# Weighted neighbour gather of one layer in two row tiles of TensorE, with other block requests, and the last residual adds of another layer on VectorE

## The reference

```python
sim  = einsum('bcp,bckp->bkp', cn, pn)              # nine similarities of a position
wts  = exp(top_sim) * mask;  wts = wts / sum(wts)   # the kept ones
out  = einsum('bckp,bkp->bcp', pat_sorted, wts)     # the neighbour gather
enhanced = out + _group_norm(x, gn_weight, gn_bias)
h    = relu(einsum('oi,bihw->bohw', w1, enhanced) + b1)
ffn  = einsum('oi,bihw->bohw', w2, h) + b2
return enhanced + ffn
```

## Time and profile before

| | |
|---|---|
| median of 3 runs | 6431.01 us (6427.97 to 6432.96) |
| profiled execution, own time | 6428.9 us |
| its span, first to last instruction | 6426.9 us |
| mean granted TensorE clock | 0.909 of full |
| layer 1, phases 0 to 4 with the weights between them | about 2584 to 3832 us of the span |
| PE / DVE / ACT / POOL busy | 82% / 66% / 37% / 40% of the span |

### The profile page before, as it was taken

One profiled execution on the slowest core, in us unless ns is written; L12 is line 12 of the kernel. 1 busy time (PEld: TensorE's weight loads), 2 busy tenths in 40 slices (PEclk: granted clock), 3 DMA queues, 4 the chain that ended last, 5 costly groups with the idle time before them and its releaser, 6 DMA issues. The chain is left out here.

```text
span 6426.9 us, 129253 instructions
## 1 busy us (share of the span) xinstructions
PE 5265.2 (82%) x49774; PEld 4307.3 (67%) x49774; DVE 4264.0 (66%) x7220; ACT 2377.9 (37%) x4272; POOL 2582.3 (40%) x1460
## 2 busy tenths in 40 slices
PE   2878787878787877156859587999979999999997
PEld 1656565656555555044647465777779999999997
DVE  5767677777676767567768658999833333455565
ACT  1666666656565665122323126665510000000000
POOL 1535454445354544245747457888800000000021
PEclk9989898888898988588979798999989999999998
DMA  3000000000000000222223110110140000000034
GB/s 134 15 28 15 28 28 15 28 28 17 27 21 22 27 17 16 85 69 67 91 71 100 40 63 15 50 47 37 36 150 0 0 0 0 0 0 0 0 52 131
DMA packets 215659, 252.28 MB, mean 39 GB/s; under 512 B 157216, under 2 KB 158496, under 8 KB 208032
## 3 DMA queue, kind: packets, MB, share of 16 engines
q1 hardware_dynamic: 83872, 229.30, 10.2%
q10 hardware_dynamic: 131328, 16.78, 1.7%
HBM read 139.49 MB, written 67.11 MB: 32 GB/s over the span
## 5 line engine op out<-in xcount | busy, mean ns | idle before, releaser
L2332 DVE SCALAR_TENSOR_TENSOR l_state<-l_conv,l_state 128x256 f32 x500 | 292.4, 585 | 794.7 <-PE l_conv L2257 794.7
L527 POOL TENSOR_TENSOR l_probs<-l_probs,l_inv 128x1024 f32<-128x1024 f32 x256 | 493.0, 1931 | 567.9 <-DVE l_inv L937 567.3
L1438 PE MATMUL l_gather_ps<-l_wdiag,l_stage 128*128 128x128 f32 x4608 | 546.9, 279 | 163.9 <-DVE l_wdiag L1593 163.8
L1438 PEld LDWEIGHTS l_gather_ps<-l_wdiag,l_stage 128*128 128x128 f32 x4608 | 536.9, 195 | 208.0 <-issue 150.1
L2257 PE MATMUL l_conv<-l_carry_hi,l_taps_hi 128*128 128x248 f32 (+2 forms) x4500 | 628.5, 284 | 38.3 <-DVE l_carry_hi L2317 38.3
L2296 POOL TENSOR_TENSOR l_state<-l_state,l_xres 128x2048 f32<-128x2048 f32 x8 | 37.1, 4670 | 1475.7 <-DVE l_carry_lo L2319 1475.7
L2257 PE MATMUL l_conv<-l_carry_lo,l_taps_hi 128*128 128x248 f32 (+2 forms) x4500 | 622.8, 283 | 7.4 <-DVE l_carry_lo L2319 7.4
L2257 PE MATMUL l_conv<-l_carry_hi,l_taps_lo 128*128 128x248 f32 (+2 forms) x4500 | 627.7, 285 | 0.0
L2257 PEld LDWEIGHTS l_conv<-l_carry_hi,l_taps_hi 128*128 128x128 f32 x4500 | 580.4, 191 | 41.8 <-DVE l_carry_hi L2317 41.7
L2109 DVE SCALAR_TENSOR_TENSOR l_acc<-l_xpad,l_w,l_acc 128x1024 f32<-128x1024 f32 x448 | 574.5, 1289 | 14.8 <-ACT l_acc L2010 1.3
L1929 POOL TENSOR_TENSOR l_sum<-l_sum,l_prod 128x1024 f32<-128x1024 f32 x224 | 538.9, 2406 | 111.0 <-ACT l_prod L2026 92.3
(11 more groups left out here) (293 smaller groups left out, 9856.7 us busy)
## 6 DMA issues: line engine op xcount, KB each, us to landing
l_xleft<-l_xt SPq DMA_DIRECT2D x64, 283.5 KB
l_xright<-l_xt SPq DMA_DIRECT2D x64, 283.5 KB
stat_xs<-in_x SPq DMA_DIRECT2D x8, 2048.0 KB, 23.1
l_hats<-in_x SPq DMA_DIRECT2D x8, 2048.0 KB, 7.7
l_xraw<-in_x SPq DMA_DIRECT2D x8, 2048.0 KB, 8.6
after_layer<-l_xraw SPq DMA_DIRECT2D x64, 256.0 KB, 2.0
l_xblk<-after_layer SPq DMA_DIRECT2D x32, 512.0 KB, 4.6
l_xres<-after_layer SPq DMA_DIRECT2D x32, 512.0 KB, 4.4
```

Source lines behind the costliest of these rows:

```text
L527: pool.tensor_tensor(part, part, inv[:, u, cols].rearrange("c (j o) -> c j o", o=1).to_broadcast([C, 4, KEYS]), ALU.mult).then_inc(scaled_ ...
L1438: last = pe.matmul(gather_ps[u][y // 4][:, y % 4 * C:(y % 4 + 1) * C], stage[:, u, y + k // 3, :], wdiag[:, y % SLOTS, k, :], start=(k == ...
L2332: dve.scalar_tensor_tensor(row, conv[h][:, 0:HB * W].rearrange("c (b w) -> c b w", b=HB), 0.0, row, op0=ALU.max, op1=ALU.add).then_inc(lin ...
```

## The change

Layer 1:

- **Gather by source row.** A block's ten rows of `stage` are now ten sources s; source s feeds the target rows `targets(s)`, one (s = 0, 9), two (1, 8) or three (2 to 7). For each of three column shifts and each image there is one product: stationary are the 64 partitions of that image in `stage`, moving is a band matrix of 64 x (64 per target row). Image 0 uses the upper and image 1 the lower 64 rows of the array, and each writes a bank of its own: 60 products a block with 64, 128 or 192 columns, 120 records.
- **Builds** are all on DVE (L1636 of the new kernel), ten a block with 192, 384 or 576 elements, each source with a place of its own; POOL builds nothing. `wsrc` is kept in another layout, filled over a cleared `wout`.
- **Group norm term on PE.** `affine` (L1453 of the new kernel) opens each bank with one product of 512 columns, `gdiag` (scales on the diagonal) times `xsum`, a separate load of the same x as `xres`. `gn_affine` goes; `enhance` is now on ACT, which only adds the shift, and `put_stage` also goes from DVE to ACT.
- **SP** requests block c+1 (and `xsum` of c+1) in step c, in front of the shifts of block c; block 0 of the next phase before the weights.
- The mask `diag` has 3 x 64 columns instead of 9 x 128, and is set by 6 selects instead of 18.

Layer 3: the left halves of images 0 to 3 are added by DVE, two pieces of 1024 elements behind each of four of the last five steps, and POOL's four adds go.

```diff
-            def gather(t, c, u, rows):
...
-                    for k in range(K2):
-                        last = pe.matmul(gather_ps[u][y // 4][:, y % 4 * C:(y % 4 + 1) * C], stage[:, u, y + k // 3, :],
-                                         wdiag[:, y % SLOTS, k, :], start=(k == 0), stop=(k == K2 - 1))
+            def affine(t, c, u):
...
+                for b in range(2):
+                    last = pe.matmul(gather_ps[u][b][:, :], gdiag[:, b, :], xsum[:, u, b, :], start=True, stop=False)
+                last.then_inc(sum_begun, 1)
...
+                    pe.wait_ge(diag_built, g * SOURCES + (s + 1))
+                    first, final = targets(s)
+                    for dx in range(3):
+                        for b in range(2):
+                            at = slice(64 * b, 64 * b + 64)
+                            last = pe.matmul(gather_ps[u][b][:, (s - 2 + first) * W:(s - 1 + final) * W], stage[at, u, s, :],
+                                             matrices(s)[at, dx, :, :].rearrange("p j x -> p (j x)"), start=False,
+                                             stop=(s == SOURCES - 1 and dx == 2))
...
+            def put_stage(t, c, u):
...
+                wait(act, row_done, (g - 1) * SOURCES)
+                act.activation(stage[:, u, :, :], rows_of(t - 1, c * ROWS, SOURCES), ACT.Copy).then_inc(staged, 1)
+            def enhance(t, c, u):
...
+                act.wait_ge(row_done, (g + 1) * SOURCES)
+                    act.activation(enh[:, u, b, :], gather_ps[u][b][:, :], ACT.Identity, bias=gshift[:, n:n + 1]).then_inc(enh_ready, 1)
...
+            def build(t, c, *sources):
...
+                    wait(dve, row_done, (g - 1) * SOURCES + (s + 1))
+                    dve.tensor_tensor(matrices(s),
+                                      diag[:, :, :].rearrange("p d (o x) -> p d o x", o=1).to_broadcast([C, 3, n, W]),
+                                      wsrc[:, first:final + 1, :, bass.ds(c * ROWS + s, 1)].rearrange("p j d o -> p d j o")
+                                      .to_broadcast([C, 3, n, W]), ALU.mult).then_inc(diag_built, 1)
...
                 def step(c, u):
-                    if t < PAIRS:
-                        load_block(t, c, u)
+                    if not (isinstance(c, int) and c == STEPS - 1):
+                        if t < PAIRS:
+                            load_block(t, c + 1, 1 - u)
+                        if t >= 1:
+                            load_sum(t, c + 1, 1 - u)
                     if t >= 1:
                         load_res(t, c, u)
                     if t < PAIRS:
                         shift(t, c, u)
...
             for steps, parts in stretches():
+                if parts[0] == (1, 3, STEPS[3] - LEAD) and len(parts) == 1:
+                    dve.wait_ge(lo_ready[0], BEFORE[3] + STEPS[3] + 1)
+                    for q in range(LEAD):
+                        step(1, 3, STEPS[3] - LEAD + q)
+                        if q < HB:
+                            add_left(2 * q, 2 * q + 1)
+                    continue
```

More of the change, by code:

```diff
@@ L1194, in layer1 @@
         turn_ps = [mem.psum("turn_ps")]
-        gather_ps = [[mem.psum(f"gather_ps{u}{half}") for half in range(2)] for u in range(2)]
+        gather_ps = [[mem.psum(f"gather_ps{u}{b}") for b in range(2)] for u in range(2)]
         hid_ps = [mem.psum(f"hid_ps{h}") for h in range(2)]
@@ L1241, in rows_of, with targets, matrices @@
             return xt[:, t % 2, bass.ds(r, n), :]
+        def targets(s):
+            return max(0, 2 - s), min(2, SOURCES - 1 - s)
+        def matrices(s):
+            widths = [targets(r)[1] + 1 - targets(r)[0] for r in range(SOURCES)]
+            start = sum(widths[:s]) * 3 * W
+            return wdiag[:, start:start + widths[s] * 3 * W].rearrange("p (d j x) -> p d j x", d=3, x=W)
         def apart(eng, at):
@@ L1253, in block_before, with steps @@
             return (t - 1, c - lag + STEPS) if isinstance(c, int) and c < lag else (t, c - lag)
-        def steps(eng, t, step):
+        def steps(eng, t, step, end=0):
             def body(j):
@@ L1262, in steps @@
                 body(j)
-            with eng.Fori(peeled, STEPS // 2) as j:
+            with eng.Fori(peeled, STEPS // 2 - end) as j:
+                body(j)
+            for j in range(STEPS // 2 - end, STEPS // 2):
                 body(j)
@@ L1313, in step @@
                         store(*block_before(t, c, 2), u)
-                steps(sp, t, step)
+                if t == 0:
+                    load_block(0, 0, 0)
+                steps(sp, t, step, 1)
                 if t < PAIRS:
+                    if t < PAIRS - 1:
+                        load_block(t + 1, 0, 0)
+                    load_sum(t + 1, 0, 0)
                     sp.wait_ge(cols_ready, t + 1)
@@ L1552, in step @@
                     g = (t - 1) * STEPS - 1 + c
+                    if t >= 1:
+                        put_stage(t, c, u)
+                    if before:
+                        enhance(*block_before(t, c, 1), 1 - u)
                     if t < PAIRS:
@@ L1586, in _, with scales @@
             link = chain.link
[L1588 removed]
+            def build(t, c, *sources):
                 g = (t - 1) * STEPS + c
[L1590 to L1611 removed]
+                for s in sources:
+                    first, final = targets(s)
+                    n = final + 1 - first
+                    wait(dve, row_done, (g - 1) * SOURCES + (s + 1))
[3 more added lines that the diff above has]
+                                      .to_broadcast([C, 3, n, W]), ALU.mult).then_inc(diag_built, 1)
+            def scales(t):
+                wait(dve, row_done, (t - 1) * STEPS * SOURCES)
+                for b in range(2):
+                    n = 2 * (t - 1) + b
+                    last = dve.tensor_scalar(gdiag[:, b, :], sh.ident[:, :], gscale[:, n:n + 1], None, ALU.mult)
+                last.then_inc(gdiag_ready, 1)
             def stats(t, c, u):
@@ L2184, in layer3 @@
         right_added = mem.sem("right_added")
-        left_added = [mem.sem(f"left_added{h}") for h in range(HALVES)]
+        left_added = mem.sem("left_added")
         stored = mem.sem("stored")
@@ L2296, in _ @@
                 pool.tensor_tensor(half, half, xres[:, b % SLOTS, :, :], ALU.add).then_inc(right_added, 1)
-            for b in range(HB):
-                pool.wait_ge(lo_ready[0], BEFORE[3] + STEPS[3] + 1)
-                pool.wait_ge(res_loaded[b % SLOTS], 16 * ((B + b) // SLOTS + 1))
-                half = state[:, b, :, 0:MID]
-                pool.tensor_tensor(half, half, xres[:, b % SLOTS, :, :], ALU.add).then_inc(left_added[0], 1)
         @block.vector
@@ L2361, in _ @@
             dve.wait_ge(lo_ready[1], BEFORE[3] + STEPS[3] + 1)
-            dve.wait_ge(right_added, B)
-            for b in range(HB, B):
-                dve.wait_ge(res_loaded[b % SLOTS], 16 * ((B + b) // SLOTS + 1))
-                for r in (0, H // 2):
-                    half = state[:, b, r:r + H // 2, 0:MID]
-                    dve.tensor_tensor(half, half, xres[:, b % SLOTS, r:r + H // 2, :], ALU.add).then_inc(left_added[1], 1)
+            add_left(*range(2 * HB, 2 * B))
 def program(nc, x, table, w, out):
```

157 lines of the change are left out of this document (69 added, 88 removed).

## The result

| | before | after |
|---|---|---|
| median, us (lowest to highest) | 6431.99 (6427.97 to 6435.11) | 6372.34 (6368.89 to 6372.94) |
| ratio after / before | | 0.9906, 95% interval 0.9889 to 0.9924 |
| span of the profiled execution | 6426.9 | 6371.0 |
| start of layer 1's setup sums to the first gather | 227.3 | 182.4 |
| first gather of phase 1 to first gather of phase 4 | 842.0 | 862.5 |

The kernel became 60 us faster, not 178: the forecast of 6254 us and its range (6205 to 6305) were wrong. The lower four lines come from the timelines of TensorE: the small products of the group sums at 2562.86 and 3837.00 us before and at 2562.82 and 3776.38 after, and the first gather records of phases 1 and 4 (2790.13 and 3632.09 before, 2745.22 and 3607.73 after).

What follows compares the result with a forecast made beforehand. Bounds in layer 1: a load (phase 0), TensorE and the chain behind `square` (1 to 3), TensorE (4), weights between phases. Gains 90 + 6 + 36 + 38 + 5 + 1.5 = 176.5 us gave 6252.4, median 6254.5; range 6205 to 6305.

Steps and rivals of the forecast that it cites:

- Setup, phase 0 and phase ends ahead of phase 1: Before phase 1: setup gains 5 us, phase 0 38 us by earlier block loads, its phase end 1.5 us.
- The gather and TensorE's step: Layer 1: gather 8.3 us a block instead of 16.8; TensorE's step 20.6 us, 18.5 in phase 4.
- A change of shape: TensorE in layer 1: tile shape changes eight times a step at 0.2 us each, 1.6 us.
- Phase 4: Layer 1's last phase: seven intervals and a last step gain some 4.5 us each, 36 us.
- The chain behind `square`: Phases 1 to 3: source 7's build follows sums needing `square`; TensorE waits 2.6 us, step 23.1 us.
- Sources 8 and 9 are built while 7 and 8 are multiplied: Phases 1 to 3, behind source 7: these builds add no further wait to the 23.1 us step.
- the tiles in turn: Rival, layer 1 gather: two 64-row tiles run one after the other, 16.7 us a block; 6444 to 6488 us; chance 0.03.
- TensorE waits for nothing: Rival, phases 1 to 3: sums come in time, step 20.6 us, 50 us more gain, 6204 us; chance 0.12.
- VectorE is the bound: Rival, phases 1 to 3: ten builds each lose 0.6 us to GpSimd, step 25 us, total 6292 us; chance 0.17.
- The shifts' landing: Rival, phase 0: shifts landing beside the loads hold it at 15 us a block, total 6275 us; chance 0.08.
- Layer 3: End of the kernel, DMA queues full: nearly no gain, 0 to 4 us, taken as 1.5 us.

Runs made afterwards that it cites:

- experiment 8: Changed kernel with only phase 0's blocks requested again at their own step instead of one step in front: 6411.1 us, measured once.
- experiment 1: Changed kernel with VectorE's builds of sources 7 to 9 ahead of the three sums instead of behind them: 6223.63 us, ratio to before 0.9673.
- experiment 2: Changed kernel, order kept, with GpSimd's two products of a block held until VectorE has built source 9 of the step before: 6320.7 us.
- experiment 7: Kernel before with one, then two useless VectorE sums of 1.1 us added among each block's three sums: 6443.8 and 6480.3 us, measured once each.
- experiment 6: Version of experiment 5 with one useless VectorE sum of 1.1 us added among its three sums: 6222.7 us, measured once.
- experiment 5: Experiment 1's order, with sources 0 to 2 of the next step also built ahead of the sums: 6207.87 us, ratio to before 0.9648.
- experiment 9: Changed kernel with layer 3 as in the kernel before, GpSimd adding the left halves in long adds: 6370.7 us, measured once.

## Why the prediction was wrong

*Setup, phase 0 and phase ends ahead of phase 1* (forecast 44.5 us): 44.9. TensorE's small product came 5.3 us earlier, its first turn 5.0 (5.0 forecast), a block took 11.5 us (12.2), with VectorE as the new bound. Right, and experiment 8 shows the cause. That the sum fits so closely is partly luck: the seven block intervals gained 42 us and not 38, and the phase end lost 1.7 instead of gaining 1.5, since the wide products that now stand ahead of the first gather take 3.7 us at the 1.2 GHz level.

*The gather and TensorE's step*: right. In phase 4 the pairs of 64-row records begin 7 ns apart, one pair of 192 columns 0.163 us after the other: 0.081 a record, forecast 0.080. Records of 128 and 64 columns cost 0.056, forecast 0.053. A change of shape costs 0.2 as forecast, half of it in front of the first record of the new shape and half behind that record, and records of 512 columns 0.43. The sum is 18.65 us against 18.5, and 20.7 against 20.6 in the first step of phases 2 and 3. Phase 4 gained 36.3 of 36 us.

*The chain behind `square`*: the wait for source 7 was 2.74 us, forecast 2.6. Right as well.

*What follows that wait*: here the prediction failed, in two steps.
- "Sources 8 and 9 are built while 7 and 8 are multiplied" put the builds behind source 7 at their price alone. GpSimd's adds were charged to source 7 with 0.6 us, and its products to nothing. The three builds took 5.52 us, and source 9 began 3.96 us behind the start of source 7 instead of 1.75: 2.2 us a step. Experiment 1 takes it away, experiment 2 takes away the products' part.
- The standstill was priced at its own length. The prediction itself put 2.6 us of idle time into a step and left the clock at the full level; the trace before gave no warning, since that kernel kept its clock through 1.97 us in each step. Source 9 at the low level cost 0.8 us more in each step, and what ran low in the next step 4.3 us (1.80, 1.33 and 1.16 by the start to start times above) in the steps of 30.7 us, less in the others.

With both, 20.7 + 2.74 + 2.2 + 0.8 + 4.3 = 30.7 us, as measured. Eighteen steps between gathers have these waits. The builds' part is 18 x 2.2 = 40 us. The clock's part is the larger: 18 x 0.8 = 14 us in source 9, and what a step has above 26.4 us, 18 in phase 1, 17 in phase 2 (1.0, 1.8, 4.2, 4.3, 3.6, 1.8) and 19 in phase 3, together 54, so 68 us. The two aren't independent: whether the clock would have fallen for less without the second wait is open (experiment 7). The three last steps with the weights took 92.8 us in the mean, 3.0 above the forecast, 9 in all (not taken apart further), and the first steps of phases 2 and 3, forecast like the others, were 2.4 us better each. That is 112 of the 115 us that phases 1 to 3 lack.

Small slips of the sums changed nothing: TensorE's terms add up to 20.5 us and not 20.6, those of the tiles in turn to 28.9 at the low end and not 29.1, and 6204, the time of the rival in which TensorE waits for nothing, lies just outside the range that was said to hold it.

*The rivals.* "VectorE is the bound" had the right ingredient, builds that each meet GpSimd, but spread it over ten builds and added it to VectorE's total. In phases 1 to 3 VectorE was never the bound: it stood idle 9.88 us in a step of 30.7, and experiments 1 and 6 bear it out. What counted was which builds met GpSimd, and who waited for these. The rule cited there, the Trainium skill, SBUF — State Buffer, Who interferes with whom, is borne out: builds end just after GpSimd's instruction, while the sums, with one input, keep 3.47 us for three with GpSimd busy beside them (experiment 1, adds at 3124.91) or not. By that rule alone a step's path could have been drawn: three two-input builds behind GpSimd's 5 us of products. The shifts' landing, the tiles in turn and "TensorE waits for nothing" did not occur; the last is what experiment 5 reaches, 6207.9 us against 6204.

*Layer 3*: 1.5 us forecast, nothing found (experiment 9).

## What to carry to other kernels

Where an instruction of VectorE both releases GpSimd's next work and stands ahead of something that TensorE waits for, put the latter first, the more so where the former itself waits for a third engine, as the sums here did for `square`: the same instructions in another order were worth 149 us here (experiment 1 against the changed kernel), more than the change itself. Contention between two engines has no average price; draw the moment at which each one's work is released, and see who is waiting then. And a forecast that leaves TensorE waits in every step like those seen here has to carry a second term for its clock, even where the trace before kept it at full.
